# Causal attention on one core: the value matmuls of two steps issued together behind every second step, and the accumulator copied one step later

## The reference, cut to what matters

```
Q, K, V = x @ Wq.T, x @ Wk.T, x @ Wv.T            # split into 16 heads of 16
p   = exp(Q K^T / 4 - running row maximum), causal # online softmax over key blocks of 128
O   = (p V) / (row sum of p)
x   = layernorm(x + O @ Wo.T)
x   = layernorm(x + int8_matmul(quantise(x), quantise(ffn_rhs)) * scales)
```

## Time and profile before

| | |
|---|---|
| three runs | 1112.25, 1116.22, 1116.11 us; median 1116.11 |
| profiled execution | 1110.95 us, of which the span of the trace is 1109.1 us |
| busy: PE, DVE, ACT, POOL | 1006.8, 822.5, 691.9, 263.3 us |
| groups 1 to 6, each | about 113 us (the fifth from 579.66 to 692.62 us) |
| group 7 | 142.0 us, from 804.60 us |
| group 8 up to its end part | from 946.62 us on |

### The profile page before, as it was taken

One profiled execution on the slowest core, in us unless ns is written; L12 is line 12 of the kernel. 1 busy time (PEld: TensorE's weight loads), 2 busy tenths in 40 slices (PEclk: granted clock), 3 DMA queues, 4 the chain that ended last, 5 costly groups with the idle time before them and its releaser, 6 DMA issues.

```text
span 1109.1 us, 20004 instructions
## 1 busy us (share of the span) xinstructions
PE 1006.8 (91%) x6280; PEld 391.3 (35%) x6280; DVE 822.5 (74%) x1083; ACT 691.9 (62%) x1471; POOL 263.3 (24%) x435
## 2 busy tenths in 40 slices
PE   8999899999999999899899999999998899999972
PEld 5565433333333333233333333333333232344321
DVE  4577776777676767668767776777788898589797
ACT  3444576767666767567666766776665465777730
POOL 4444401020102010120112011201111100555543
PEclk9999999999999999999999999999999899999995
DMA  5666400012011201120102010201021240235501
GB/s 162 208 184 212 121 12 2 7 35 68 5 33 35 65 5 36 31 68 8 35 11 80 14 35 4 81 20 35 6 69 35 73 81 1 46 97 145 154 29 48
DMA packets 71786, 66.39 MB, mean 60 GB/s; under 512 B 15112, under 2 KB 65608, under 8 KB 71684
## 3 DMA queue, kind: packets, MB, share of 16 engines
q1 hardware_dynamic: 71684, 65.10, 21.0%
HBM read 43.25 MB, written 21.35 MB: 58 GB/s over the span
## 4 chain that ended last, share of the span: by engine, by line
PE 72%; DVE 19%; issue 3%; ACT 3%; DMA 1%; POOL 1%; SPq 1%; POOLq 0%; DVEq 0%; ACTq 0%
PE ps_acc L694 22%; PE ps_max L668 20%; PE ps_score L713 18%; DVE block_max L941 11%; PE ps_score L587 5%; PE ps_score L594 2%; ACT PR L893 2%; PE ps_max L671 2%; DVE stats L1055 1%; DMA end_slots<-heads_out 1%; PE ps_acc L568 1%; DVE end_slots L1065 1%; DVE amax L1074 1%; PE ps_max L768 1%; DVE V L1065 0%
## 5 line engine op out<-in xcount | busy, mean ns | idle before, releaser
L941 DVE TENSOR_REDUCE block_max<-ps_max 128x2 f32<-128x1024 f32 (+3 forms) x640 | 655.9, 1062 | 234.8 <-PE ps_max L668 160.2
L893 ACT ACTIVATE PR<-ps_score 128x512 f32<-128x512 f32 (+3 forms) x1280 | 602.7, 536 | 273.0 <-PE ps_score L713 267.7
L713 PE MATMUL ps_score<-QS,KS 99*128 99x512 bf16 (+3 forms) x1280 | 378.5, 352 | 26.6 <-ACT PR L893 18.8
L668 PE MATMUL ps_max<-KS,QS 96*128 96x512 bf16 (+3 forms) x1280 | 358.3, 350 | 41.2 <-DVE block_max L941 38.2
L694 PE MATMUL ps_acc<-PR,VG 128*32 128x512 f32 (+3 forms) x2560 | 301.6, 543 | 0.0
L713 PEld LDWEIGHTS ps_score<-QS,KS 99*128 99x128 bf16 x1280 | 108.2, 97 | 339.7 <-ACT PR L893 236.9
L668 PEld LDWEIGHTS ps_max<-KS,QS 96*128 96x128 bf16 x1280 | 120.7, 98 | 161.0 <-DVE block_max L941 82.0
L1163 POOL TENSOR_SCALAR_AFFINE_SELECT PR<-PR 128x512 f32<-128x512 f32 x128 | 81.3, 636 | 331.5 <-ACT PR L893 331.5
L671 PE MATMUL ps_max<-mask_q,ident_b 128*128 128x128 bf16 x512 | 102.8, 221 | 0.0
L694 PEld LDWEIGHTS ps_acc<-PR,VG 128*32 128x32 f32 x2560 | 50.6, 108 | 95.9 <-ACT PR L893 52.9
L1171 POOL CAST max_parts<-neg_max 16x128 bf16<-16x128 f32 (+1 forms) x31 | 8.8, 283 | 273.0 <-ACT neg_max L876 272.1
(11 more groups left out here) (122 smaller groups left out, 475.3 us busy)
## 6 DMA issues: line engine op xcount, KB each, us to landing
QS<-qparts SPq DMA_DIRECT2D x192, 64.0 KB, 2.3
KS<-kparts SPq DMA_DIRECT2D x192, 64.0 KB, 2.3
qparts<-end_slots SPq DMA_DIRECT2D x16, 384.0 KB, 5.2
kparts<-end_slots SPq DMA_DIRECT2D x16, 384.0 KB, 5.7
PR<-in_L_attn_x SPq DMA_DIRECT2D x8, 512.0 KB, 4.4
heads_out<-accS SPq DMA_DIRECT2D x124, 32.0 KB
end_slots<-in_L_attn_x SPq DMA_DIRECT2D x4, 512.0 KB, 9.7
out_y<-end_slots SPq DMA_DIRECT2D x8, 256.0 KB, 2.1
```

The source lines that it names most:

```text
L668: m = pe.matmul(bank[:, 0:w], QS[0:STACK, p, i // TPC, j, i % TPC * P:i % TPC * P + P], KS[0:STACK, p, b, j, 0:w], start=True, stop=not diag)
L713: pe.matmul(bank[:, 0:CH - s], KS[:, p, kb // TPC, j, kb % TPC * P:kb % TPC * P + P], QS[0:KROWS, p, c, j, s:CH], start=True, stop=True).t ...
L893: act.activation(PR[:, k % 4, j, 0:w], ps_score[:, score_slot(pos), 0:w], ACT.Exp, scale=SCALE).then_inc(s_exp, 1)
L941: dve.tensor_reduce(block_max[:, h * PAIR:h * PAIR + PAIR, i, b], ps_max[:, slot_at:slot_at + PAIR, 0:w], AX.X, ALU.max).then_inc(s_reduce ...
```

## The change

In `group` of the tensor engine, values are no longer issued in every step. Behind an odd step k stand now the values of step k - 3 and of step k - 2, in this order and with nothing between them; behind an even step stand none. BATCH = 2 is the number of steps that go together. Since every chunk ends with an odd step, the last values of a chunk stand where they stood, behind kb = 1 of the next chunk. On ACT the copy of the accumulator moves from behind the last exponential of kb = 1 to behind the second exponential of kb = 2. Nothing is added to or taken from what is computed.

```diff
-    LAG = 2
+    LAG, BATCH = 2, 2
+    assert NS % BATCH == 0 and all((n + 1) % BATCH == 0 for n in LAST)
...
-                        if k >= LAG:
-                            values(g, k - LAG, kind)
-                        elif not first:
-                            values(g - 1, NS + k - LAG, KIND(g - 1))
+                        for back in range(LAG + BATCH - 1, LAG - 1, -1) if k % BATCH == BATCH - 1 else ():
+                            if k >= back:
+                                values(g, k - back, kind)
+                            elif not first:
+                                values(g - 1, NS + k - back, KIND(g - 1))
...
-                            if kb == 1 and j == HG - 1 and c >= first:
+                            if kb == BATCH and j == 1 and c >= first:
                                 copy_acc(g if c else g - 1, (c - 1) % CHUNKS)
```

## The result

| | before | after |
|---|---|---|
| median | 1114.18 us (four runs, 1110.75 to 1116.22) | 1139.27 us (four runs, 1132.38 to 1145.10) |
| ratio to before | | 1.0222, 95% interval 1.0165 to 1.0279 |
| profiled span | 1109.1 us | 1136.0 us |

The change makes the kernel 2.2% slower, some 25 us. Slower was the likeliest case of the prediction, but 1123 us were forecast and 1135 was the end of the range.

A forecast was written before the change was run, and what follows sets the result against it. PE was taken as the bound (busy 91%, 72% of the chain), DVE nearly so in the seventh group. +2.4 + 6.5 - 1.2 = +7.7 us; taking +7 on the 1116.11 median gave 1123 us, range 1098 to 1135.

The forecast's parts named there:

- the likeliest case: Whole kernel: slower, around 1123 us; with the costlier-copy rival it held chance 0.50; by itself 1117 to 1132 us.
- The price of a burst, 0.23 us for each merge: PE's values: joining two steps' bursts saves 0.23 us of issue, between 0.145 and 0.235; 36.6 us over 159 merges.
- The gain is lost to waits for DVE and ACT in the longer stretch: Full pair, steps 28 and 29: the 0.23 us saved goes, 0.19 to DVE's item slot, the rest to ACT waits.
- The sum of a group, +0.4: First six groups: the twenty pairs' differences add to +0.4 us a group, 2.4 for six.
- 28/29: Pair of full steps 28 and 29 in each of the first six groups: forecast -0.02 us.
- 20/21: Pair of steps 20 and 21 in each of the first six groups: forecast +0.05 us.
- 18/19: Pair of steps 18 and 19, small items following one another, first six groups: forecast -0.47 us; DVE keeps up.
- The moved copy: ACT's accumulator copy: 0.48 us enters the dense stretch; full pair 6.00 us instead of 5.67, three times a group.
- The seventh group, +6.5: Seventh group: DVE spaces the items; twelve full pairs give +7.0 us, eight with narrow steps about -0.5.
- The eighth group, -1.2: Eighth group, no items, PE waits for layernorms and a load: -1.2 us, between 0 and -4.6.
- I give it a fifth of its merges: Eighth group: a fifth of its merges reach the span, 5 x 0.23 = -1.2 us.
- The range: Whole kernel: 1098 to 1135 us for 8 in 10; six groups at 2 us each and the seventh uncertain.

The follow-up runs named there:

- e5: Kernel before (values in every step) with DVE reducing only half the columns of each item; ratio 0.9584 to the kernel before, fifth group 108.26 us.
- e6: Changed kernel (values together, copy moved) with DVE reducing only half the columns; ratio 0.9596 to the kernel before, fifth group 108.42 us.
- e8: Kernel before with both DVE's reductions and ACT's exponentials halved; ratio 0.9495 to the kernel before, fifth group 106.85 us.
- e9: Changed kernel with both DVE's reductions and ACT's exponentials halved; ratio 0.9241 to the kernel before, fifth group 103.05 us.
- e11: Kernel before with ACT taking only half the columns of each exponential; ratio 0.9918 to the kernel before, fifth group 111.60 us.
- e12: Changed kernel with ACT taking only half the columns of each exponential; ratio 1.0016 to the kernel before, fifth group 112.69 us.
- e1: Values together in all groups, but the accumulator's copy back at its old place behind kb = 1; ratio 1.0222 to the kernel before.
- e2: Values in every step as in the kernel before, only the accumulator's copy moved behind kb = 2's second exponential; ratio 1.0075 to the kernel before.
- e3: Values together and copy moved in the eighth group alone; ratio 1.0036 to the kernel before.
- e4: Values together and copy moved in the first six groups alone; ratio 1.0153 to the kernel before, fifth group 115.17 us.
- e7: Values together only in eight chosen pairs of the first six groups, copy at its old place; ratio 0.9917 to the kernel before, median 1104.17 us.
- e10: As e7, with values also together in five pairs of the seventh group; ratio 0.9914 to the kernel before.

## Why the prediction was right or wrong

- **The price of a burst, 0.23 us for each merge: right.** The long burst takes 1.86 us, and with nobody to wait for a pair gains 0.24. The Trainium skill's drain on a change of the tiling mode ("TensorEngine Tiling (Array Packing)", Key Properties) fits this. The values also differ from the scores in type, fp32 for bf16, but in the eighth group before a projection in fp32 that isn't column-tiled begins 0.44 us after the first of two scores (1002.11 to 1002.55), which is what two scores take, so that change of type alone costs nothing on the way in. No run tries the tiling apart. The same page's warning that emptying PSUM may become the bottleneck (PSUM Bottleneck) describes what then happens.
- **The gain is lost to waits for DVE and ACT in the longer stretch: right** in mechanism and in sign for the first six groups, shown by e5, e6, e8, e9, e11 and e12. In 17 of 20 pairs the working with a few durations came within 0.16 us.
- **The sum of a group, +0.4: mis-sized; it is +2.2**, 13 us in six groups instead of 2.4. This is the larger of the two terms that failed. Three pairs make 1.33 of the 1.8 missing. In 28/29 and 20/21 I had left DVE's combining of the block maxima out of its queue, which delays the next reduction by 0.3: an estimate of 0.6 us a group. In 20/21 two narrow diagonal items wait as well. The rest of these two pairs, 0.4, and the 0.4 of 18/19 with its seven items are not taken apart; that 18/19 gains 0.29 with the exponentials halved (e12 against e11) says that ACT is in it.
- **Half clock in the six groups: put at nothing.** The profile has 16.8 us there, 3.2 of them in the two stretches in pair 20/21.
- **The moved copy: roughly right.** Some 0.3 was forecast for each of three full pairs; e1 shows 0.14, 0.33 and only 0.04 there (6/7, 14/15, 26/27), and 0.28 in 2/3. That the moved copy would be free in a kernel without the merge (said in the expectation of e2, not in the prediction) was wrong.
- **The seventh group, +6.5: the profile has +1.9.** But the kernel before had a stretch of 6.8 us at half clock there, in pair 20/21, which by itself is 3.0 us shorter after the change. The other 19 pairs add to +4.9. In e1, which has such a stretch in the same pair as the kernel before, the seventh group is 4.5 longer. So like for like the forecast was 2 us too high, and the clock makes it look worse.
- **The eighth group, -1.2: wrong in sign.** It is 7.4 us longer in the changed kernel and 3.8 in e3. The other step that failed is "I give it a fifth of its merges": I counted PE's saving in a part in which PE is waited for, and didn't ask what stands behind a wait when both steps' values come after it. (A fifth of 20 merges is also 4 and not 5, which changes 0.2.) In pair 22/23 of e3 that order is worth 0.85, a later input 1.2 and the clock 1.6. The changed kernel is another 3.6 longer than e3, of which 2.3 are in its first two pairs (+1.10 and +2.03 against +0.40 and +0.42), where its granted clock was at half for 6.8 us:

```profile
969.40:976.20 6.80, 6.45 (x33) 3.61 (x33) 0.00 (x0) 3.78 (x14) 6.34 (x13) 0.50 0.11 24
```

- **TensorE's clock: not in the sum.** In the eighth group the granted clock is 0.94 of full speed instead of 0.99. The four runs of the changed kernel had a mean clock of 0.984, 0.975, 0.974 and 0.972 and took 1132.38, 1137.78, 1140.76 and 1145.10 us in this order. The fastest, with a clock as good as the profile of before (0.981), is still 21 us slower than that one, so what goes with the clock adds up to 7 us to the median and doesn't explain the rest.
- **The range**: I took 2 us of error in each of the first six groups as the far end, 12 in all. The pairs' error was 1.8 in each, all of one sign, because the pattern and what was left out of it repeat; with the clock it came to 14.4. Bounds of a repeated part don't average out. What then carried the result past 1135 is the eighth group, for which I had allowed -4.6 to 0 and which is 8.6 above its forecast, against 4.6 that the seventh came out better.

## What to carry to other kernels

Work that feeds no other engine, between work that does, is also the pause in which those engines empty their queues. Before putting such pieces together, compare the longer stretch with the depth of each queue (here 3 banks and 2 slots) at each consumer's pace, and put every instruction of the consumer into that sum, the short ones too. Where the pattern repeats exactly, one trace of "all together" tells place by place where it pays, and choosing those places gave 0.8% where doing it everywhere cost 2.2%.

## What the runs showed of the hardware

Two bursts of column-tiled fp32 matmuls joined cost 0.21 to 0.25 us less than apart where no wait took it (e9 against e8), at widths from 128 to 512 columns. Two windows of 3.4 us in the third group show TensorE's clock (the third number from the end): first the changed kernel, with 0.51, then the kernel before at the same time, with 1.00.

```profile
416.40:419.80 3.40, 3.27 (x20) 0.94 (x20) 0.83 (x3) 0.00 (x0) 0.00 (x0) 0.51 0.02 5
```

```profile
416.40:419.80 3.40, 2.85 (x24) 1.31 (x23) 2.51 (x3) 2.35 (x5) 0.00 (x0) 1.00 0.37 100
```

That fall came in pair 20/21, in which PE waits twice for item slots (0.36 and 0.73 us in the fifth group), and cost 1.6 us (2.10 against 0.54 in other groups). In e1 it came in that pair in each of the first three groups. Over the first six groups of the traces with this pair together and whole reductions (the changed kernel, e1, e4, e12) it came in 8 of 24; with the pair apart (before, e2, e3, e5, e7, e8, e10, e11) in none of 48. In e3 and in the changed kernel another followed the wait of 2.2 us in step 23 of the eighth group. What exactly decides it was not tried.
